# Attention output: one VectorE product into a buffer and an accumulating transfer, in place of four products that add onto x

## The reference

```
x = x + 0.5 * ffn(layernorm(x))
x = x + attn(layernorm(x))
x = x + 0.5 * ffn(layernorm(x))

attn, for each of 16 heads:
  q, k, v = complex projections, 64 wide; q and k rotated by the position
  E = exp(clip(-mu * |i - j|, -30, 0))
  maha = max(|q|^2 + E^2 |k|^2 - 2 E Re(q conj k), 0) / V(E)
  logits = coef * log1p(maha / nu) - 32 * log(V), causal
  A = softmax(logits)
  out = sum over heads of (A @ v) @ Wo
```

## Time and profile before

| | |
|---|---|
| time, median of 3 runs | 1686.04 us (1684.88 to 1686.15) |
| the profiled execution: its time, its span | 1685.38 us, 1683.6 us |
| PE busy, share of the span | 1624.1 us, 96% |
| DVE | 1494.5 us, 89% |
| ACT | 1443.1 us, 86% |
| POOL | 1013.6 us, 60% |
| L1609, `accumulate` | 512 instructions, 149.4 us in all |
| L1500, `rotate` | 127 instructions, 303.7 us in all, 421.4 us of POOL's idle time ahead of them |

### The profile page before, as it was taken

The page is one execution under the profiler, slowest core; times in us unless marked ns, Lnnn a source line. Parts: engine busy times, 40 slices in busy tenths (PEclk is TensorE's granted clock), DMA queues, the critical chain, the costliest instruction groups (busy, mean ns, idle before and its releaser), DMA issues. The chain is left out here.

```text
span 1683.6 us, 31247 instructions
## 1 busy us (share of the span) xinstructions
PE 1624.1 (96%) x9690; PEld 1227.8 (73%) x9690; DVE 1494.5 (89%) x3380; ACT 1443.1 (86%) x2909; POOL 1013.6 (60%) x954
## 2 busy tenths in 40 slices
PE   5999988999999999999999999999999999899998
PEld 4787865777776777677777777777776776677876
DVE  6878878999999999999999999999999989977665
ACT  6677678999999999999999999999999998765765
POOL 3564556666666666665766666666666656245555
PEclk9999999999999999999999999999999999999999
DMA  6000022232223323232222323232232322100000
GB/s 178 1 1 1 1 97 73 64 92 64 76 70 76 79 64 85 58 82 70 75 74 64 92 64 76 55 92 69 74 84 60 80 59 51 26 8 7 13 13 13
DMA packets 50484, 100.05 MB, mean 59 GB/s; under 512 B 8208, under 2 KB 25872, under 8 KB 50320
## 3 DMA queue, kind: packets, MB, share of 16 engines
q1 hardware_dynamic: 50320, 98.07, 22.7%
HBM read 17.95 MB, written 5.24 MB: 14 GB/s over the span
## 5 line engine op out<-in xcount | busy, mean ns | idle before, releaser
L1500 POOL TENSOR_TENSOR early<-early 128x1024 f32<-128x1024 f32 x127 | 303.7, 2391 | 421.4 <-PE pS L1191 227.6
L661 POOL TENSOR_TENSOR hid_lo_d<-hid_d,hid_hi_d 128x512 fp32r<-128x512 f32 x176 | 231.4, 1315 | 218.4 <-ACT hid_hi_d L566 211.8
L1392 ACT ACTIVATE early<-early,qnorm 128x128 f32<-128x128 f32 (+3 forms) x512 | 246.6, 552 | 68.0 <-DVE early L1591 67.3
L1191 PE MATMUL pS<-early 128*128 128x128 f32 (+3 forms) x1024 | 297.6, 433 | 0.4 <-PEq L115 0.4
L1376 ACT ACTIVATE early<-early,nmax 128x128 f32<-128x128 f32 (+3 forms) x512 | 280.9, 558 | 7.7 <-DVE nmax L1578 7.4
L1191 PEld LDWEIGHTS pS<-early 128*128 128x128 f32 x1024 | 164.7, 191 | 96.1 <-issue 61.4
L1587 DVE SCALAR_TENSOR_TENSOR pS<-pS,ek 128x1280 f32<-128x1280 f32 x128 | 190.9, 1492 | 43.5 <-PE pS L1191 41.9
L1509 POOL TENSOR_TENSOR ek<-early 128x128 f32<-128x128 f32 (+3 forms) x256 | 216.1, 877 | 3.0 <-ACT early L1384 2.6
L1509 POOL TENSOR_TENSOR ek<-decay,early 128x128 f32<-128x128 f32 (+3 forms) x256 | 215.0, 873 | 0.0
L1233 PE MATMUL pS<-ident,early 128*128 128x128 f32 x1280 | 184.9, 278 | 13.3 <-DVE early L1591 7.0
L1405 ACT ACTIVATE early<-early,params 128x512 f32<-128x512 f32 (+1 forms) x256 | 196.4, 816 | 0.0
(11 more groups left out here) (393 smaller groups left out, 3752.5 us busy)
## 6 DMA issues: line engine op xcount, KB each, us to landing
early<-early SPq DMA_DIRECT2D x263, 256.0 KB, 3.4
early<-trig_d SPq DMA_DIRECT2D x64, 64.0 KB, 2.0
trig_d<-early SPq DMA_DIRECT2D x3, 1024.0 KB, 6.9
early<-in_w SPq DMA_DIRECT2D x3, 704.0 KB, 8.7
x_sb<-in_x SPq DMA_DIRECT2D x4, 512.0 KB, 8.3
early<-in_wqk SPq DMA_DIRECT2D x16, 128.0 KB, 3.4
cos<-trig_d SPq DMA_DIRECT2D x32, 64.0 KB, 2.2
sin<-trig_d SPq DMA_DIRECT2D x32, 64.0 KB, 2.0
```

What stands on the lines that cost most here:

```text
L661: g.tensor_tensor(hid_lo[:, par], hid[:, par], hid_hi[:, par].bitcast(F32), ALU.subtract).then_inc(lo_done, 1)
L1191: last = pe.matmul(s.pS[:, span(I)], rot[:, I * P:(I + 1) * P], rot[:, N:N + (I + 1) * P], start=True, stop=True)
L1392: last = a.activation(u[:, span(I)], u[:, span(I)], ACT.Relu, bias=qnorm[:, r % 2, I:I + 1])
L1500: g.tensor_tensor(rot[:], by_cos[:], crossed[:], ALU.add).then_inc(S["rot_done"], 1)
```

## The change

`accumulate` is taken apart. DVE multiplies the whole bank by the reciprocals in one instruction, into a new buffer `weighed` (`normalise_out`), all of it ahead of `distances` and no longer half ahead and half behind. It waits until the transfer of the pair before has landed. POOL waits for that product at the beginning of its step and begins a transfer that adds `weighed` onto the four tiles of x (256 KB). `acc_done` counts landed transfers now, by 16; `weigh` on PE waits for the product (`y_done`) and not for the sum. `moments` waits for the landed sum. `q_turned` moves into free columns of `dist`, which makes room for the new buffer.

```diff
-        q_turned = sb("q_turned", [P, 2, P])
+        q_turned = s.dist[:, 2 * N:SW].rearrange("p (k d) -> p k d", k=2)
+        weighed = sb("weighed", [P, TILES, P])
...
-                wait(pe, S["acc_done"], n)
+                wait(pe, S["y_done"], n)
...
+            def accumulate(i, r):
+                n, b = i * 16 + r, r % B
+                g.wait_ge(S["y_done"], n + 1)
+                xb = s.x_sb[:, b * TILES:(b + 1) * TILES, :]
+                g.dma_start(xb, weighed[:], accum_op=ALU.add).then_inc(S["acc_done"], 16)
+
             def a_step(i, r):
+                if live(i, r - 3):
+                    accumulate(i, r - 3)
                 if live(i, r + 1):
                     if (i, r) != (0, -1):
                         rotate(i, r + 1)
...
-            def accumulate(i, r, tiles=range(TILES)):
-                n, b = i * 16 + r, r % B
+            def normalise_out(i, r):
+                n = i * 16 + r
                 v.wait_ge(S["av_done"], n + 1)
                 v.wait_ge(S["rinv_done"], n + 1)
-                for I in tiles:
-                    xt = s.x_sb[:, b * TILES + I, :]
-                    last = v.scalar_tensor_tensor(xt, s.p7[:, I * P:(I + 1) * P], rinv[:, r % 4, I:I + 1], xt,
-                                                  ALU.mult, ALU.add)
-                if TILES - 1 in tiles:
-                    last.then_inc(S["acc_done"], 1)
+                wait(v, S["acc_done"], 16 * n)
+                v.tensor_tensor(weighed[:], s.p7.rearrange("p (c d) -> p c d", c=TILES),
+                                rinv[:, r % 4, :].unsqueeze(2).broadcast_to([P, TILES, P]), ALU.mult).then_inc(S["y_done"], 1)
 
             def moments(r, n):
                 b = r % B
-                v.wait_ge(S["acc_done"], n + 1)
+                v.wait_ge(S["acc_done"], 16 * (n + 1))
...
                 if n == PAIRS:
-                    accumulate(i, r - 3)
+                    normalise_out(i, r - 3)
...
                     if live(i, r - 3):
-                        accumulate(i, r - 3, range(TILES // 2))
+                        normalise_out(i, r - 3)
                     distances(i, r)
...
-                if live(i, r - 3) and n != PAIRS:
-                    accumulate(i, r - 3, range(TILES // 2 if live(i, r) else 0, TILES))
+                if live(i, r - 3) and n > PAIRS:
+                    normalise_out(i, r - 3)
```

More of the change, by code:

```diff
@@ L1831, in program @@
                  "ek_done s_done w_done t_done relu_done ln_done zred_done exp_done v_done "
-                 "qt_done val_done tr_done trc_done av_done rinv_done acc_done stat_done dve_passed pool_passed sp_passed "
+                 "y_done qt_done val_done tr_done trc_done av_done rinv_done acc_done stat_done dve_passed pool_passed sp_passed "
                  "late_stat late_mv late_var late_ln late_root late_rstd late_step late_xn late_xt late_hi late_lo mv_done expanded0 expanded1")
```

## The result

The changed kernel takes 1728.74 us (median of four, 1727.26 to 1729.33), the kernel before 1686.10 in the same comparison: a ratio of 1.0253, 95% interval 1.0235 to 1.0271, +42.6 us. Forecast were 1713 and a range of 1669 to 1770. The profiled execution has a span of 1727.5 us, 43.9 more than before.

What follows compares the result with a forecast made beforehand. It took PE to bound even attention steps and DVE odd ones, with PE right behind. 1685.4 + 14 (odd steps) + 13 (tail) = 1712.4, on the median 1713 us; range for 8 in 10: 1669 to 1770.

Steps and rivals of the forecast that it cites:

- +14 in odd steps: 59 odd attention steps: POOL held by the issue, `rotate` late, each 9.04 us against 8.80, +0.24 per step.
- 0 in even ones: Even attention steps: PE ends last and DVE only idles longer, so they stay at 9.86 us.
- +13 in the tail: Last eight pairs: `moments` waits for the landed sum; +5 over steps 123 to 127, -0.4, +8.5 in 129 and 130.
- Slower, and why: Whole kernel: slower than before, chance 0.73, because POOL held by the issue runs late and `spread` meets `peaks`.
- What `peaks` would show: Odd steps: the first two reductions of `peaks` at 0.8 and 1.0 us.
- G: Time for which the accumulating transfer's issue holds POOL: taken as 1.05 us, between 0.46 and 2.39.
- The rule (lateness plus 7.77): Odd step lasts `rotate`'s lateness after `distances` plus 7.68, plus 0.09 for the longer product: 1.27 + 7.77 = 9.04 us.
- The saving on DVE: One 512-column product replaces four of 128: 0.39 us saved per step, buying nothing as `peaks` comes 0.4 sooner and meets `spread`.
- The floor of rival 1: Shortest odd step if POOL stays on time: 8.43 us, 0.37 below the mean odd step.
- rival 1: Faster: the issue doesn't hold POOL (about 0.2 us), 59 odd steps gain 0.37 each, tail +7: 1669 us; chance 0.19.
- G + L: Accumulating transfer from issue to landing: POOL's hold of 1.05 us plus 3.4 us until landed.
- Landing hidden elsewhere: Ahead of the last eight pairs: the next product, a step later, never waits for the landing, 4.8 us in all.

Runs made afterwards that it cites:

- no_issue: Changed kernel with VectorE adding the last eight pairs; for the other 120 POOL waits for the product but begins no transfer, their addition left out: 1683.29 us.
- sp_copy: Changed kernel with VectorE adding the last eight pairs; for the others SP plainly copies the same 256 KB onto x, POOL only waits: 1683.00 us.
- between: Changed kernel with VectorE adding the last eight pairs; POOL begins the other transfers between `rotate` and `spread` instead of ahead of `rotate`: 1695.63 us.

## Why the prediction was right in sign and 16 us short

- *Where the 16 us are*: forecast were +14 in odd steps, 0 in even ones and +13 in the tail; the traces show +26.9, +6.4 and +9.8, and 0.8 in the second dense phase.
- *Slower, and why*: right. POOL in order, held by the issue, `spread` meeting `peaks`: `no_issue`, `sp_copy` and `between` show it.
- *What `peaks` would show*: the first reduction at 0.8, right (0.84); the second at 1.0, wrong (0.61).
- *The product*: 0.69 forecast, 0.68 measured, 0.61 from start to start. Right.
- *The hold of POOL*: G was taken as 1.05; from start to start it is 0.68. The issue was to begin at 0.22; it begins at 0.37. So `rotate` starts at 1.05 instead of 1.27. But its row is longer, and it ends 1.00 later than in the earlier trace rows (3.68 after `distances`, for 2.69), where the forecast had 0.97. The lateness was about right, by two errors that cancel: luck.
- *The odd step*: the step that failed. The rule (lateness plus 7.77) would give 8.82 for 1.05, and gave 9.04 for 1.27; measured is 9.28, so the term of +14 was +26.9. The rule's constant, 7.68, came from one step of before, late by 1.95, in which two reductions are held. The trace of before has two steps whose lateness is nearer to the forecast, 1.10 and 1.35; in them the first reduction alone is held, and the step is the lateness plus 7.92 in both (columns as in the earlier trace rows; the next `distances` of the first is at 966.52):

```profile
957.50 1.49 DVE L1587 SCALAR_TENSOR_TENSOR pS<-pS,ek 128x1280 f32<-128x1280 f32 x1
...
958.60 2.38 POOL L1500 TENSOR_TENSOR early<-early 128x1024 f32<-128x1024 f32 x1 [3.50 <-DMA early<-early]
...
963.78 0.67 DVE L1578 CUSTOM_DVE_ANT_0 early<-early,lam,params 128x128 f32<-128x128 f32 x1
...
1264.65 1.48 DVE L1587 SCALAR_TENSOR_TENSOR pS<-pS,ek 128x1280 f32<-128x1280 f32 x1
...
1266.00 2.39 POOL L1500 TENSOR_TENSOR early<-early 128x1024 f32<-128x1024 f32 x1 [3.54 <-DMA early<-early]
...
1270.92 0.92 DVE L1578 CUSTOM_DVE_ANT_0 early<-early,lam,params 128x128 f32<-128x128 f32 x1
...
1273.92 1.48 DVE L1587 SCALAR_TENSOR_TENSOR pS<-pS,ek 128x1280 f32<-128x1280 f32 x1
```

  With 7.92 in place of 7.68 the forecast's own 1.27 gives 1.27 + 7.92 + 0.09 = 9.28, some +28 us; this is reckoned after the event. The constant isn't one number: what is held depends on which piece of `spread` the reductions meet.
- *The saving on DVE*: the prediction said that it buys nothing, which was right, but for a reason that was wrong: `peaks` didn't come 0.4 sooner. It starts at 6.27 or 6.28 in 58 of the 59 odd steps of the kernel before, the changed kernel, `no_issue` and `between`, held by ACT's logs. The prediction read the end of the logs' first half rightly (5.9; it is 5.96), but left out the 0.31 from there to `peaks`, and "no gap" on DVE overlooked the 0.14 ahead of `peaks`.
- *The floor of rival 1*: 8.43 was wrong twice, 8.78 by the logs and 8.65 by TensorE with the product moved. With an issue that costs nothing the kernel takes 1683 (`no_issue`), and that leaves out the tail; with its 9.8 it would be some 1693 (an estimate), not 1669. Rival 1 had no room to be true.
- *Even steps worth 0*: missed by 6.4 us. The prediction asked only whether `rotate` is late enough to pass PE; it didn't ask what else on DVE meets `spread`. The weight pieces do (0.39 to 1.57 and 0.27 to 0.97).
- *The Trainium skill's exclusion* (SBUF — State Buffer, Who interferes with whom) is agreed with, as far as these rows show it: the reductions and L1559, each with two SBUF inputs, stretch beside `spread`, 0.35 to 0.84 and 0.39 to 1.57.
- *The tail*: +13 forecast, +9.8 measured, the mechanism as told. Mis-sized was G + L: 4.45, measured 3.3 from issue to landing, the issue included (steps 123 to 126 +2.9 for +4, from step 127 on +6.9 for +9). The Trainium skill's fit (DMA: Bandwidth & Descriptors, Anatomy of one DMA) gave 2.6 as an estimate for the same; the trace lies between.
- *Landing hidden elsewhere*: right; DVE waits for it in no step ahead of the last eight.

## What to carry to other kernels

An accumulating transfer isn't free because "DMA does it": its issue is an instruction of POOL, and what stands behind it in POOL's order starts 0.68 us late here and ends up to 1.0 us late. Before moving work off an engine, find what starts the next thing on it (here ACT's logs and TensorE's scores): time that is freed ahead of a wait for another engine is not won. And a rule about one engine disturbing another, taken from a single slow step, should be checked against the other slow steps of the trace, the nearest to the forecast first, and for all instructions that can meet, not for the one where it was seen.

## What the runs showed of the hardware

- An accumulating transfer of 256 KB from SBUF onto SBUF lands 3.3 us after its issue starts; the plain copy from SP between the same buffers (`sp_copy`) lands after 2.3 (columns as in the earlier trace rows). The hold of POOL is about the same for 128 KB (0.61 each from start to start) as for 256 KB (0.68).

```profile
x_sb<-weighed SPq DMA_DIRECT2D x120, 256.0 KB, 2.3
```

- Beside POOL's products a CAST with one SBUF input stretched too, from 0.27 to 0.97 us on average (L1553).
- TensorE's clock fell in the tail. In step 130 PE had waited 4.22 us for DVE, did 1.12 us of transposes, and then ran at a granted clock of 0.50, the 1.2 GHz level, so that a product of 512 columns took 0.63 us for the 0.39 of 1504.97 (timeline of PE, then the stretch, columns as in the earlier trace rows):

```profile
1504.97 0.39 PE L74 MATMUL pQK<-xT_hi,w_hi 128*128 128x512 f32 x1
...
1514.50 1.12 PE L1297 MATMUL pV<-ident,early 128*128 128x128 f32 x4 [4.22 <-DVE early L1736]
...
1517.55 0.63 PE L74 MATMUL pS<-xT_hi,w_hi 128*128 128x512 f32 x1
```

```profile
1515.00:1520.00 5.00, 3.18 (x9) 2.07 (x8) 1.30 (x9) 0.00 (x0) 0.86 (x1) 0.50 0.30 52
```
